# An AdaLN block on one core: maxima packed anew, the turn of the maxima and the projection moved in TensorE's order, and the root by log and exp

## The reference, cut to what matters

```python
h = layernorm(x) * (1 + ca) + sa            # x is 2 x 1024 x 128; the six modulations come from silu(c) @ wmod
x = x + ga * attention(h)                   # 16 heads of 8; q, k rotated; k and v from a latent of 64
#   scores = q k^T / sqrt(8), masked by pages of 32 tokens: a query sees the keys of its own and of earlier pages
#   softmax over keys, times v, times wo
h = layernorm(x) * (1 + cb) + sb
x = x + gb * ffn(h)                         # 4 rounds of a mixture: 4 experts (128 -> 512 -> 128, tanh gelu), top 2 of 4
```

## The kernel before, in words

| scores of unit | 0 | 1 | 2 | 3 | 4 | 5 | 6 | 7 | 8 | 9 |
|---|---|---|---|---|---|---|---|---|---|---|
| its columns a head | 512 | 512 | 256 | 512 | 512 | 512 | 512 | 512 | 512 | 256 |
| bin before: columns a head | 512 | 512 | 512 | 512 | 512 | 512 | 256 | 512 | 384 | 384 |
| bin before: pieces | 2 | 1 | 1 | 1 | 1 | 2 | 2 | 4 | 2 | 2 |
| bin after: columns a head | 512 | 512 | 256 | 512 | 512 | 512 | 512 | 512 | 512 | 256 |
| bin after: pieces | 1 | 1 | 2 | 2 | 1 | 2 | 2 | 1 | 4 | 2 |

## Time and profile before

### The profile page before, as it was taken

How to read it: one execution, slowest core, us unless ns; L and a number is a source line. 1 busy time by engine, 2 the same in 40 slices (tenths; PEclk the granted TensorE clock), 3 DMA queues, 4 the chain that set the end, 5 groups by cost and what they waited for, 6 DMA issues and landing times.

```text
span 738.9 us, 11087 instructions
## 1 busy us (share of the span) xinstructions
PE 664.0 (90%) x4004; PEld 445.5 (60%) x4004; DVE 570.0 (77%) x954; ACT 514.0 (70%) x914; POOL 177.6 (24%) x152
## 2 busy tenths in 40 slices
PE   3937799999999987846999999999999999999996
PEld 2413444444444434434877787777877787778785
DVE  5568878788788753375789888988888898988775
ACT  2320167787777776613888888888888888888984
POOL 0222710000000000003144244433444244422222
PEclk9975589999999999985999999999999999999999
DMA  7297001101101000000211011110111011100201
GB/s 265 87 302 239 3 1 59 46 16 61 60 1 61 3 2 3 1 0 26 89 58 58 1 58 58 59 42 16 59 59 57 2 58 58 59 20 38 73 16 28
DMA packets 16902, 40.64 MB, mean 55 GB/s; under 512 B 2832, under 2 KB 8208, under 8 KB 14736
## 3 DMA queue, kind: packets, MB, share of 16 engines
q1 hardware_dynamic: 15536, 38.20, 15.0%
q10 hardware_dynamic: 1312, 1.74, 0.7%
HBM read 32.19 MB, written 9.57 MB: 57 GB/s over the span
## 4 chain that ended last, share of the span: by engine, by line
PE 35%; DVE 12%; issue 5%; ACT 1%; POOL 0%; POOLq 0%; DVEq 0%
DVE gel_lo L1017 7%; PE y L920 6%; PE y L922 6%; PE y L921 6%; PE hid L910 5%; PE hid L911 5%; PE hid L909 5%; PE plog L931 2%; DVE part L1073 1%; ACT gel_hi L985 1%; DVE at_least L1045 1%; PE pcw L940 1%; DVE cw L1064 0%; DVE cw L1062 0%; DVE dl L1052 0%
## 5 line engine op out<-in xcount | busy, mean ns | idle before, releaser
L1017 DVE TENSOR_TENSOR gel_lo<-gel,gel_hi 128x512 fp32r<-128x512 f32 x256 | 248.3, 1010 | 6.7 <-ACT gel_hi L985 5.7
L557 ACT ACTIVATE probs<-st 128x512 f32<-128x512 f32 (+1 forms) x320 | 160.3, 554 | 90.8 <-PE st L693 87.5
L590 DVE TENSOR_REDUCE mcol<-mx 128x2 f32<-128x1024 f32 (+3 forms) x160 | 176.0, 1118 | 40.7 <-PE mx L712 38.2
L984 ACT ACTIVATE gel<-hid,b_sb 128x512 f32<-128x512 f32 x256 | 176.1, 688 | 39.7 <-PE hid L911 17.0
L985 ACT ACTIVATE gel_hi<-hid,b_sb 128x512 fp32r<-128x512 f32 x256 | 174.7, 683 | 0.0
L1125 POOL TENSOR_TENSOR cur<-cur,part 128x512 f32<-128x512 f32 x64 | 106.4, 1662 | 251.9 <-DVE part L1073 251.9
L712 PE MATMUL mx<-ks,qs 30*128 30x128 f32 (+4 forms) x576 | 91.4, 397 | 20.3 <-PEq L219 12.5
L920 PE MATMUL y<-gel_hi,w_hi 128*128 128x512 f32 x256 | 104.5, 408 | 0.4 <-DVE gel_lo L1017 0.4
L909 PE MATMUL hid<-cur_hi,w_hi 128*128 128x512 f32 x256 | 102.7, 401 | 0.0
L910 PE MATMUL hid<-cur_lo,w_hi 128*128 128x512 f32 x256 | 102.5, 401 | 0.0
L911 PE MATMUL hid<-cur_hi,w_lo 128*128 128x512 f32 x256 | 102.3, 400 | 0.0
(11 more groups left out here) (141 smaller groups left out, 564.9 us busy)
## 6 DMA issues: line engine op xcount, KB each, us to landing
cwb<-gate_rows SPq DMA_DIRECT2D x16, 1024.0 KB, 4.6
ks<-k_rows SPq DMA_DIRECT2D x8, 512.0 KB, 3.7
qs<-q_rows SPq DMA_DIRECT2D x8, 512.0 KB, 4.5
q_rows<-pieces_q SPq DMA_DIRECT2D x12, 256.0 KB, 4.4
k_rows<-pieces_k SPq DMA_DIRECT2D x12, 256.0 KB, 4.6
x_sb<-in_x SPq DMA_DIRECT2D x4, 256.0 KB, 4.7
k_rows<-in_k_rows SPq DMA_DIRECT2D x1, 1024.0 KB, 8.3
q_rows<-in_q_rows SPq DMA_DIRECT2D x1, 1024.0 KB, 10.9
```

The source lines that it names most:

```text
L557: nc.scalar.activation(probs[k % PROBS][:, h, 0:n], st[:, (HG * k + h) % ST_RING, 0:n], ACT.Exp, scale=SCALE).then_inc(exp_done, 1)
L590: nc.vector.tensor_reduce(mcol[g % 2][:, PAIR_HEADS[pair]:PAIR_HEADS[pair] + 2, slot:slot + step * (len(blocks) - 1) + 1:step], mx[:, at % ...
L984: nc.scalar.activation(gel[n % RING][:, :], hid[n % RING][:, :], ACT.Gelu_apprx_tanh, bias=bias)
L1017: nc.vector.tensor_tensor(gel_lo[n % RING][:, :], gel[n % RING][:, :], gel_hi[n % RING][:, :], ALU.subtract).then_inc(lo_ok, 1)
```

## The change

It makes five edits. (1) The bins have a new order and other blocks: tile 2's and tile 6's keys are cut in 256 and 128 rather than 384, and `mcol` gets three slots for each tile (24), preset to +3e38 by two memsets on GpSimd, for which VectorE waits once. (2) `merge` becomes one TENSOR_REDUCE over the three slots, 128x32 out of 128x96, into a tile `mmin`. (3) The turn of the maxima goes behind `weigh`. (4) `project` goes between the two quads of a step. (5) sqrt and reciprocal become exp(-0.5 ln(v)), with ln and exp on ScalarE and a semaphore between them.

```diff
 BINS = [
-    ([(0, 0), (4, 512)], 128, 0, 8),
-    ([(1, 0), (5, 512)], 256, 1, 8),
-    ([(2, 0)], 384, 2, 1),
-    ([(6, 512)], 384, 10, 1),
     ([(3, 0)], 512, 3, 1),
     ([(4, 0)], 512, 4, 1),
+    ([(1, 0), (5, 512)], 256, 1, 12),
+    ([(0, 0), (4, 512)], 128, 0, 12),
     ([(5, 0)], 512, 5, 1),
     ([(6, 0)], 512, 6, 1),
+    ([(2, 256), (6, 768)], 128, 10, 4),
+    ([(2, 0), (6, 512)], 256, 2, 20),
     ([(7, 0)], 512, 7, 1),
-    ([(7, 512)], 512, 11, 1),
+    ([(7, 512)], 512, 15, 1),
 ]
...
     nc.vector.tensor_scalar(ve, m.mv[:, tiles, 1:2], EPS, None, ALU.add).then_inc(var_ok, 1)
-    v.wait_ge(sqrt_ok, turn + 1)
-    link(nc.vector.reciprocal(rstd, m.sd[:, tiles, :]))
+    v.wait_ge(root_ok, turn + 1)
...
+def root_step(nc, act, var_ok, log_ok, root_ok, m, tiles, turn):
+
+    act.wait_ge(var_ok, turn + 1)
+    nc.scalar.activation(m.sd[:, tiles, :], m.ve[:, tiles, :], ACT.Ln).then_inc(log_ok, 1)
+    act.wait_ge(log_ok, turn + 1)
+    nc.scalar.activation(m.rstd[:, tiles, :], m.sd[:, tiles, :], ACT.Exp, scale=-0.5).then_inc(root_ok, 1)
...
-            act.wait_ge(var_ok, 1)
-            nc.scalar.activation(m.sd[:, :, :], m.ve[:, :, :], ACT.Sqrt).then_inc(sqrt_ok, 1)
+            root_step(nc, act, var_ok, ln_ok, root_ok, m, slice(0, NT), 0)
...
-    mcol = [l.sb(f"mcol{s}", [P, HG, 12]) for s in range(2)]
+    mcol = [l.sb(f"mcol{s}", [P, HG, PARTS * JB]) for s in range(2)]
+    mmin = [l.sb(f"mmin{s}", [P, HG, JB]) for s in range(2)]
...
+            for s in range(2):
+                nc.gpsimd.memset(mcol[s][:, :, :], -MASKED).then_inc(mcol_init, 1)
...
             for b in range(B):
-                act.wait_ge(var_ok, b + 1)
-                nc.scalar.activation(m.sd[:, batch_tiles(b), :], m.ve[:, batch_tiles(b), :], ACT.Sqrt).then_inc(sqrt_ok, 1)
+                root_step(nc, act, var_ok, ln_ok, root_ok, m, batch_tiles(b), b)
...
-                nc.vector.tensor_tensor(mc[:, :, 4:8], mc[:, :, 4:8], mc[:, :, 8:12], ALU.min).then_inc(mchain, 1)
-
+                nc.vector.tensor_reduce(mmin[g % 2][:, :, :], mcol[g % 2][:, :, :].rearrange("p h (x t) -> p h t x", t=JB),
+                                        AX.X, ALU.min).then_inc(mchain, 1)
+
+            v.wait_ge(mcol_init, 2)
...
             for k in range(STEPS):
-                for pair in range(PAIRS):
-                    quad(k, pair)
+                quad(k, 0)
+                project(k - FIRST_TILE)
+                quad(k, 1)
+                if k >= 1:
+                    weigh(k - 1)
                 if turn_due(k + NU + LEAD) is not None:
                     turn_maxima(turn_due(k + NU + LEAD))
-                if k >= 1:
-                    weigh(k - 1)
-                project(k - FIRST_TILE)
             weigh(STEPS - 1)
```

More of the change, by code:

```diff
@@ L79 @@
 TURN_AFTER = 2 * PAIRS
+PARTS = 3
 PAIR_HEADS = [2, 0]
@@ L162, in adaln_block, with rstd_steps @@
             ffn(nc, m, Mem(nc, part))
-def rstd_steps(nc, v, link, var_ok, sqrt_ok, m, tiles=slice(0, NT), turn=0):
+def rstd_steps(nc, v, link, var_ok, root_ok, m, tiles, turn):
     ve, rstd, nw = m.ve[:, tiles, :], m.rstd[:, tiles, :], m.nw[:, tiles, :]
     nc.vector.tensor_scalar(ve, m.mv[:, tiles, 1:2], EPS, None, ALU.add).then_inc(var_ok, 1)
-    v.wait_ge(sqrt_ok, turn + 1)
-    link(nc.vector.reciprocal(rstd, m.sd[:, tiles, :]))
+    v.wait_ge(root_ok, turn + 1)
     link(nc.vector.tensor_tensor(nw, rstd, rstd, ALU.mult))
@@ L211, in prep @@
     exp_c, silu_c, mods, mod_read = (l.sem(n) for n in ("exp_c", "silu_c", "mods", "mod_read"))
-    var_ok, sqrt_ok, xn_ok, turn_ok, h_ok = (l.sem(n) for n in ("var_ok", "sqrt_ok", "xn_ok", "turn_ok", "h_ok"))
+    var_ok, ln_ok, root_ok, xn_ok, turn_ok, h_ok = (
+        l.sem(n) for n in ("var_ok", "ln_ok", "root_ok", "xn_ok", "turn_ok", "h_ok"))
     swap_ok, q_ok, lat_ok, lat_sb, k_ok, v_ok, v_sb = (
@@ L319, in _ @@
             link(s)
-            rstd_steps(nc, v, link, var_ok, sqrt_ok, m)
+            rstd_steps(nc, v, link, var_ok, root_ok, m, slice(0, NT), 0)
             v.wait_ge(mods, 1)
@@ L436, in attention @@
     st_done, exp_done, pv_done, ov_read = (l.sem(n) for n in ("st_done", "exp_done", "pv_done", "ov_read"))
-    bin_full, bin_read, mchain = (l.sem(n) for n in ("bin_full", "bin_read", "mchain"))
+    bin_full, bin_read, mchain, mcol_init = (l.sem(n) for n in ("bin_full", "bin_read", "mchain", "mcol_init"))
     vs_init, vs_ok, w_in, w_hi, w_lo, small_in = (
@@ L442, in attention @@
         l.sem(n) for n in ("heads_ok", "rec_ok", "att_ok", "back_ok", "att_sb", "add_ok", "x_ok"))
-    dve, var_ok, sqrt_ok, xn_ok, ht_ok, h_ok = (
-        l.sem(n) for n in ("dve_proj", "var2_ok", "sqrt2_ok", "xn2_ok", "ht_ok", "h2_ok"))
+    dve, var_ok, ln_ok, root_ok, xn_ok, ht_ok, h_ok = (
+        l.sem(n) for n in ("dve_proj", "var2_ok", "ln2_ok", "root2_ok", "xn2_ok", "ht_ok", "h2_ok"))
     CHAIN = 3
@@ L510, in take_apart @@
             def take_apart(g):
-                mc = mcol[g % 2]
-                nm = mc[:, :, 0:JB]
+                nm = mmin[g % 2][:, :, :]
                 hi, lo = mpc[:, :, 0, :], mpc[:, :, 1, :]
@@ L654, in norm @@
                 link(last)
-                rstd_steps(nc, v, link, var_ok, sqrt_ok, m, batch_tiles(b), b)
+                rstd_steps(nc, v, link, var_ok, root_ok, m, batch_tiles(b), b)
                 v.wait_ge(w_lo, NE)
```

## The result

| | before | after |
|---|---|---|
| time, median of 20 runs each, side by side | 746.34 us (739.07 to 760.4) | 738.41 us (734.63 to 750.32) |
| the profiled execution's own time | 740.68 us | 735.29 us |
| its span | 738.9 us | 733.5 us |

The ratio of the times is 0.9914, 95% interval 0.9888 to 0.994. Forecast were 737.7 us and a gain of 3.0; the profiled execution gained 5.4. The forecast's own ratio, 737.7 / 740.68 = 0.996, lies just outside the interval. The ratio leaves out the executions that are over 1.5% above the fastest of their kernel.

A forecast was written before the change was run, and what follows sets the result against it. TensorE's order bounds the kernel, a chain with ScalarE's exp in it. From 740.68: -7.4 projection, 0 bins and turn, +0.7 lead, +3.75 roots give 737.7 us; range 732 to 741.5, forecast's chance 0.62.

The forecast's parts named there:

- Projection: Last twelve loop steps: projection moves into TensorE's idle gap between the quads, saving 7.4 us; bounds 0 and -11.
- Rival B: Steps 68 to 79: the gap doesn't take the projection, nothing saved, 745.1 us; chance 0.08.
- Loop: Attention loop: new bins and the later turn of the maxima cancel out, 0 us, bounds -3 to +3.
- the sum of bins and turn: Loop: six groups at +0.13 and seven unit 2s at -0.12 give 0; bounds -0.5 to +0.5 a group.
- unit 7: Loop step of unit 7: VectorE's reads delay dummies and second quad; step 3.25 us against 3.28, -0.03.
- Rival D: Loop: VectorE's short reads do open the loop, -0.5 a group over six, 734.7 us; chance 0.09.
- Lead: Lead before the first scores, paced by VectorE: the new bin order costs +0.7 us, range 0 to +1.5.
- Roots: Three roots in `prep` and `norm`: a table load between ln and exp, +3.75 us in all; bounds 0 and +7.6.
- the +1.25 of the text: Each root: exp's table load after ln, less the reciprocal, adds 1.25 us on VectorE's path.
- Rival A: Roots: one table set serves ln and exp, no load inside a root, 734.0 us; chance 0.18.
- rival C: Loop groups: maxima rows come late, seven later groups wait 1.55 us each, 748.6 us; chance 0.03.
- a clock at 0.5 later into the loop than the first 10 us: Granted clock in the loop: listed among the signs that would show the forecast wrong.

The follow-up runs named there:

- experiments 1 and 2: 1: changed kernel with the projection back at the step's end, ratio 1.0077; 2: kernel before with only the projection moved between the quads, ratio 0.9894.
- experiment 5: Changed kernel with the old bins (384 and 384, old order) in the new slots; median 748.42 us, ratio 1.0007 to the kernel before.
- experiment 6: Changed kernel with the turn of the maxima ahead of `weigh` again; median 737.92 us, ratio 0.9907 to the kernel before.
- The repeat: Changed kernel run again, unchanged; profiled span 737.4 us, ten executions with spans from 735.8 to 747.7 us.
- experiment 4: Changed kernel with one table set for ln and exp loaded by name at the start of prep and of attention; ratio 0.9823 to the kernel before.
- repeat of experiment 4: Changed kernel with the named ln and exp table set, run once more; median 736.06 us, ratio 0.9815 to the kernel before, span 736.4 us.
- experiments 7, 8 and 11: 7 and 8: one dummy per lead bin from unit 4, in changed kernel (0.9975) and with sqrt back (0.9906); 11: sqrt back, no first-group dummies, 747.38 us.

## Why the prediction was right or wrong, point by point

**Projection, -7.4 forecast, -7.93 measured in the changed kernel, -7.91 alone.** Right in place, mechanism and size. Rival B (the gap doesn't take it) falls with experiments 1 and 2. Steps 75 to 78 take 2.77, 2.77, 2.88 and 2.89, where 2.8 to 2.9 was said. The four wide steps save 3.0 and step 68 0.59, as worked out. The half microsecond that the sum lacked lies mostly in units 0, 1, 3 and 4 (steps 70, 71, 73 and 74): they save 0.57 to 0.69 each, 2.56 together, where 2.2 was forecast.

**Loop, 0 forecast, -2.23 measured.** The step that failed is the sum of bins and turn, put at 0 a period and measured at -0.21, and in it above all unit 7. Most other units came out as worked out: unit 8 at 2.86 (2.85), unit 2 at 2.41 (2.40), unit 6 at 2.67 (+0.06, as said). Unit 9 is at 2.43 (2.48), and unit 0 grew by 0.03, for which the sum had nothing. Unit 7 was put at 3.25 and is 3.06. VectorE's reads reach 0.52 into it rather than 0.6, so the dummies start at 0.54 rather than 0.65 and the second quad at 1.23 rather than 1.31. VectorE's third read then ends at 3.01 rather than 3.16, and the next quad starts 0.05 behind it rather than 0.09. A tenth of a microsecond in the links of one chain was nearly the whole difference, six times over: six periods at -0.22 are -1.3. Experiments 5 and 6 put the bins at 0.18 of a period and the turn at 0.03 to 0.06. The other 0.9 lies in step 2 of the first group (3.31 us before, 2.41 after; steps 0 and 1 took the same in both). About 0.1 to 0.2 of it is unit 2's shorter bin, the rest the clock: in both profiled executions it rose at 97.3 us, and the loop began 2.25 later in the changed one, so fewer of its steps ran at 1.2 GHz. The forecast had no term for that. The repeat, with the rise at 102.5 us, shows that the moment isn't fixed by the program; this part of the gain is luck of the two profiled executions. Rival D had the sign, at twice the amount (-0.5 a group), but not the reason, as experiment 5 shows.

**Lead, +0.7 forecast, +0.77 measured**; the old bins take it back to 31.12. Right.

**Roots, +3.75 forecast, +1.48 and +2.54 measured, 4.0 together.** Right. From the variance to the end of VectorE's Newton step in `prep` is 1.55 before and 2.78 after, +1.23 for the +1.25 of the text. With one set named (experiment 4) the same stretch takes 1.51 us, so log and exp without a load between them are no dearer than square root and reciprocal. The rest of the 1.48 is within the scatter: in the fourteen profiles of this study `prep` ends between 54.60 and 57.59 us, on the mean at 56.8 where a load stands between ln and exp (six profiles) and at 55.6 where none does (eight). Rival A is excluded by the rows for this kernel, and true for the one of experiment 4, where the set is named. The Trainium skill (ScalarE: Activation LUTs, Table sets: the hidden batching unit) says that one load is enough for ln then exp. In these runs this holds only where the program names the set: experiment 4 has no load between the two, the changed kernel has one each time. The drain that the Trainium skill gives (ScalarE: Activation LUTs, What ACT_TABLE_LOAD costs, 1.38 us) would by estimate have made each root 1.25 + 1.38 = 2.6 dearer; the trace disagrees, with 0.01 between a load's end and the activation behind it.

**Maxima rows (rival C).** The loop's first quads never wait for `mrow`; periods of 26.87 leave no room for it. From the copy's end to the next unit 0 are 5.0 us (194.44 to 199.46; 5.15 forecast), against the 4.3 that the DMAs took in the lead. Experiment 6, with the rows 1 us earlier, gains nothing.

**The forecast time.** 737.7 against 738.41 (median) and 735.29 (the profiled execution, by which the sum went). The 2.4 us between are nearly all the loop's. That the forecast lies within 0.7 us of the median is luck in part: it forecast a gain of 3.0, the profiled executions gained 5.4, and the medians of twenty lie 7.9 apart, because the kernel before came out at 746.34 beside the changed one and not at the 740.68 from which the forecast started. Of the ratio, 0.9914, a part goes with the clock: the median of the mean clocks is 0.9385 in the changed kernel's twenty executions and 0.934 in the 79 of the kernel before that were run beside the experiments. Straight lines of span over clock through the same executions give, at 0.940, 742.7 us before and 736.9 after: -5.8. It is a rough figure, as the executions come from several batches, but it says that most of the gain isn't the clock's. Whether the change itself has a part in how the clock falls, no run settles.

The mark "a clock at 0.5 later into the loop than the first 10 us" was a bad one: the unchanged repeat meets it.

**A better version.** The change with its root undone or with one table set: 0.9868 and 0.9815 against 0.9914. Only the second interval lies clear of the changed kernel's. The lowest spans are 729.0 and 729.3 us against 732.8.

## What to carry to other kernels

In a loop written out by hand, look for the row in which TensorE idles for an activation, and put there the work that stands at the end of the step: its price is then only what it needs beyond the gap. When two activation functions follow each other on the path, look for the load between them, and name a set that holds both. Compare stages between marks in the trace before comparing spans: here the moment at which the clock rose moved a span by as much as the whole change.

## What the runs showed of the hardware

**The clock's rise and fall are not the program's alone.** Twelve of the fourteen profiles have it up at some time from 96 to 118 us, one at 129 (no dummies) and one at 161 (experiment 4). The same program had it up at 97.3 and, run again, at 102.5. In experiment 6 TensorE was busy 5.00 of 5.00 us in every window from 93 to 113 with the clock at 0.50. The first and the last of these windows, and the next:

```profile
93.00:98.00 5.00, 5.00 (x35) 2.25 (x34) 2.21 (x3) 1.96 (x5) 2.01 (x2) 0.50 0.00 0
...
108.00:113.00 5.00, 5.00 (x30) 1.77 (x26) 2.45 (x2) 2.17 (x4) 0.00 (x0) 0.50 0.01 3
113.00:118.00 5.00, 5.00 (x29) 1.94 (x28) 2.62 (x3) 2.17 (x4) 0.46 (x2) 0.54 0.00 0
```

From the first scores to the first copy of the loop is 24.4 us with a rise at 97 and 33.0 here, though the copy stands 1 us sooner in its step. A second place where executions differ comes behind the last bins and dummies. Four windows of the repeat of experiment 4:

```profile
270.00:275.00 5.00, 3.63 (x28) 1.20 (x27) 0.17 (x1) 4.32 (x8) 0.46 (x2) 1.00 0.00 0
275.00:280.00 5.00, 5.00 (x30) 2.63 (x30) 0.83 (x3) 2.19 (x5) 0.00 (x0) 0.55 0.04 10
280.00:285.00 5.00, 5.00 (x32) 2.95 (x33) 0.75 (x3) 1.74 (x5) 0.00 (x0) 0.50 0.00 0
285.00:290.00 5.00, 4.89 (x45) 3.10 (x43) 2.57 (x10) 3.94 (x9) 0.00 (x0) 0.92 0.01 2
```

and the late part takes 37.63 us instead of 33.24. In the changed kernel's first profile it stayed at 1.00 there. It fell behind steps 66 and 67, in which TensorE has neither bins nor dummies nor a projection to do (busy 3.63 of 5 us in the first of these windows). Five of the fourteen profiles have such a fall, each starting between 275 and 286 us: the repeat of the changed kernel (3 us long), that of experiment 4 (10), and experiments 7, 8 and 11 (24, 20 and 27). That the light steps cause it is not shown, since all fourteen profiles have such steps and nine show no fall. Whether dummies in these two steps would keep it up wasn't tried.
